# Attention core: how far the pass over the row maxima runs ahead of the scores

## The reference

```python
scores = jnp.einsum('bhqd,bhkd->bhqk', q, k) / jnp.sqrt(jnp.asarray(hd, x.dtype))
attn = jax.nn.softmax(scores, axis=-1)
out = jnp.einsum('bhqk,bhkd->bhqd', attn, v)
```

## Time and profile before

| | |
|---|---|
| time, median of 3 runs | 4916.33 us (4907.15 to 4920.6) |
| profiled execution, its own time | 4910.83 us, span 4909.0 us |
| busy of the span | PE 85%, DVE 59%, ACT 48%, POOL 28% |
| `pyr_core`, span of its pass A and B | about 322 to 535 us |
| `l1x_core` | about 1490 to 1898 us |
| `l2a_core` | about 2312 to 2520 us |
| `l3x_core` | about 4280 to 4803 us |

### The profile page before, as it was taken

The page is one execution under the profiler, slowest core; times in us unless marked ns, Lnnn a source line. Parts: engine busy times, 40 slices in busy tenths (PEclk is TensorE's granted clock), DMA queues, the critical chain, the costliest instruction groups (busy, mean ns, idle before and its releaser), DMA issues. The chain is left out here.

```text
span 4909.0 us, 69714 instructions
## 1 busy us (share of the span) xinstructions
PE 4175.8 (85%) x20384; PEld 1981.0 (40%) x20384; DVE 2875.6 (59%) x6517; ACT 2348.4 (48%) x4572; POOL 1358.6 (28%) x1202
## 2 busy tenths in 40 slices
PE   8779856689788997897979699999998988489986
PEld 6322445386552333573334233333335544222224
DVE  4558474401667884005861378787873256388866
ACT  4447331243244774333754355454552246269993
POOL 0122141211101111112110188787883212101112
PEclk9669988799887998897989799999999989689998
DMA  8545212354033332674335422111210034623421
GB/s 288 118 101 123 52 38 35 142 198 145 25 131 67 63 63 66 246 242 135 81 83 197 150 71 66 61 61 61 69 51 24 22 113 96 152 48 92 96 55 38
DMA packets 332041, 486.56 MB, mean 99 GB/s; under 512 B 84516, under 2 KB 232596, under 8 KB 317252
## 3 DMA queue, kind: packets, MB, share of 16 engines
q1 hardware_dynamic: 325008, 449.92, 32.2%
q0 software_dynamic: 6384, 32.61, 2.1%
q10 hardware_dynamic: 348, 0.44, 0.0%
HBM read 327.63 MB, written 143.92 MB: 96 GB/s over the span
## 5 line engine op out<-in xcount | busy, mean ns | idle before, releaser
L1356 POOL TENSOR_TENSOR lc_totals<-lc_totals,lc_weights 128x1024 f32<-128x1024 f32 (+1 forms) x320 | 623.0, 1947 | 165.9 <-DVE lc_totals L1305 134.8
L1265 ACT ACTIVATE lc_weights<-ps 128x1024 f32<-128x1024 f32 x384 | 393.2, 1024 | 447.1 <-PE ps L1182 436.8
L1286 DVE TENSOR_REDUCE lc_part_max<-ps 128x2 f32<-128x1024 f32 x384 | 466.1, 1214 | 206.4 <-PE ps L1162 204.0
L1182 PE MATMUL ps<-lc_q,lc_k 64*128 64x512 f32 x1536 | 398.1, 596 | 4.8 <-issue 4.8
L1192 PE MATMUL ps<-lc_weights,lc_v 128*64 128x512 f32 x1536 | 371.7, 605 | 0.0
L866 DVE TENSOR_REDUCE l1x_core_part_max<-ps 128x1 f32<-128x512 f32 x512 | 316.4, 681 | 55.4 <-PE ps L690 55.3
L862 DVE CUSTOM_DVE_ANT_0 l3x_core_unused<-ps,l3x_core_mask_q 128x512 f32<-128x512 f32 x512 | 330.6, 686 | 6.9 <-DVE l3x_core_row_max L870 4.9
L825 ACT ACTIVATE l3x_core_weights<-ps 128x512 f32<-128x512 f32 x512 | 327.6, 694 | 7.3 <-PE ps L758 7.0
L825 ACT ACTIVATE l1x_core_weights<-ps 128x512 f32<-128x512 f32 x512 | 266.1, 603 | 84.0 <-PE ps L758 83.8
L808 ACT ACTIVATE ps<-l3x_core_mask_k 128x512 f32<-128x512 f32 x384 | 270.7, 705 | 35.9 <-DMA l3x_core_mask_k<-in_mask_k 35.9
L690 PE MATMUL ps<-l3x_core_k,l3x_core_q 96*128 96x512 bf16 x512 | 214.2, 419 | 56.0 <-DVE l3x_core_part_max L862 40.8
(11 more groups left out here) (493 smaller groups left out, 8574.1 us busy)
## 6 DMA issues: line engine op xcount, KB each, us to landing
cf_w<-in_L1f_w SPq DMA_DIRECT2D x32, 1024.0 KB, 7.5
lc_k<-latent_k SPq DMA_DIRECT2D x32, 768.0 KB, 6.6
lc_v<-latent_values SPq DMA_DIRECT2D x32, 768.0 KB, 4.9
latent_k<-feed_staged SPq DMA_DIRECT2D x64, 256.0 KB, 2.6
latent_values<-feed_staged SPq DMA_DIRECT2D x64, 256.0 KB, 2.0
k_heads<-proj_parts SPq DMA_DIRECT2D x40, 384.0 KB, 2.6
q_heads<-proj_parts SPq DMA_DIRECT2D x32, 384.0 KB, 2.6
q_heads<-proj_parts SPq DMA_DIRECT2D x32, 256.0 KB, 3.0
```

Source lines behind the costliest of these rows:

```text
L1182: mm = nc.tensor.matmul(out[j], k_tile[g % RING][strip(j), i * P:(i + 1) * P], q_tile[g % RING][strip(j), :], start=False, stop=True)
L1265: nc.scalar.activation(weights[:, i % TILES, :, :], k.ps[:, B0 + (i % 2) * HEADS:B0 + (i % 2 + 1) * HEADS, 0:nq], ACT.Exp, scale=scale).th ...
L1286: nc.vector.reduce_max(own, k.ps[:, A0:A0 + HEADS, :], AX).then_inc(a_taken, 1)
L1356: nc.gpsimd.tensor_tensor(total, total, own, ALU.add).then_inc(added_by_pool, 1)
```

## The change

In stages with 16-channel heads that are neither causal nor cut into spans (`pyr_core`, `l1x_core`, `l2a_core`, `l3x_core`), pass A runs one group and three key tiles ahead in place of two groups (`EARLY = 3`). FRONT is 12 chunks for both sizes; the turn of the maxima comes at key tile TURN = nkt - 3 (1 for 512 keys, 5 for 1024), within it after the third head. `split_max` moves behind `normalise` in POOL's group, `row` to the end of SP's group (with a mask in group 3: before the last of the four mask tiles), and the mask rows for the next batch are loaded in group 2 in place of group 1. The other two stages keep their order.

```diff
-    def chunks_of(i):
-        some = list(range(i * NCH // nkt, (i + 1) * NCH // nkt))
-        return [some[len(some) * j // heads:len(some) * (j + 1) // heads] for j in range(heads)]
+    EARLY = 3 if small and not causal and spans is None else nkt
+    late_row = EARLY < nkt
+    FRONT, TURN = NCH * EARLY // nkt, nkt - EARLY
+    def chunks_at(s):
+        return [(1 + m // NCH, m % NCH) for m in range(FRONT + s * NCH // NS, FRONT + (s + 1) * NCH // NS)]
...
 SP, group(b, g):
-                if exists(*later(b, g, 1)):
+                if exists(*later(b, g, 1)) and not late_row:
                     row(*later(b, g, 1))
...
-                if mask is not None and g == groups - 3 and exists(b + 1, 0):
+                if mask is not None and g == groups - (2 if late_row else 3) and exists(b + 1, 0):
...
+                new_mask = mask is not None and g == groups - 1 and exists(b + 1, 0)
+                for i in range(nkt // 2 if new_mask else 0):
+                    if late_row and i == nkt // 2 - 1:
+                        row(*later(b, g, 1))
+                    sync.wait_ge(exp_done, at(b, g, NS, 2 * (i + 1) * heads + 3))
+                    load_mask_k(b + 1, i)
+                if exists(*later(b, g, 1)) and late_row and not new_mask:
+                    row(*later(b, g, 1))
...
 PE (DVE alike, with maxima for pass_a and negate for turn):
-            pass_a(0, 1, range(NCH))
+            pass_a(0, 1, range(FRONT))
...
-                        pass_a(*later(b, g, 2), more[j])
+                        for ahead, n in chunks_at(s):
+                            if exists(*later(b, g, ahead)):
+                                pass_a(*later(b, g, ahead), [n])
+                        if late_row and (i, j) == (TURN, heads - 2) and exists(*later(b, g, 1)):
+                            turn(*later(b, g, 1))
...
-                    if i == 0 and exists(*later(b, g, 1)):
+                    if not late_row and i == 0 and exists(*later(b, g, 1)):
                         turn(*later(b, g, 1))
...
 POOL, group(b, g):
-                    if small and i == 0 and exists(*later(b, g, 1)):
+                    if small and not late_row and i == 0 and exists(*later(b, g, 1)):
                         split_max(*later(b, g, 1))
...
                 if g >= 2 and to_finish(b - 1):
                     normalise(b - 1, 2 * g - 4)
                     normalise(b - 1, 2 * g - 3)
+                if late_row and exists(*later(b, g, 1)):
+                    split_max(*later(b, g, 1))
```

More of the change, by code:

```diff
@@ L745, in group @@
                 for i in range(nkt):
-                    more = chunks_of(i) if exists(*later(b, g, 2)) else [()] * heads
                     qs, ks = queries_of(i), slice(i * P, (i + 1) * P)
@@ L910, in _ @@
             negate(0, 0)
-            maxima(0, 1, range(NCH))
+            maxima(0, 1, range(FRONT))
             def group(b, g):
@@ L915, in group @@
                 for i in range(nkt):
-                    more = chunks_of(i) if exists(*later(b, g, 2)) else [()] * heads
                     for j in range(heads):
                         after = step_after(b, g, i * heads + j)
+                        if late_row and (i, j) == (TURN, heads - 1) and exists(*later(b, g, 1)):
+                            negate(*later(b, g, 1))
                         if after[2] in by_vector and exists(*after[:2]):
                             fill(*after, at(b, g, NS, i * heads + j + 3))
-                        maxima(*later(b, g, 2), more[j])
+                        for ahead, n in chunks_at(i * heads + j):
+                            if exists(*later(b, g, ahead)):
+                                maxima(*later(b, g, ahead), [n])
                         if (i, j) in inverse_at and not small and exists(*before):
                             invert(*before, inverse_at.index((i, j)))
-                    if i == 0 and exists(*later(b, g, 1)):
+                    if not late_row and i == 0 and exists(*later(b, g, 1)):
                         negate(*later(b, g, 1))
```

## The result

The changed kernel takes 4979.5 us (median of 4 runs, 4975.7 to 4980.9), the kernel before 4915.6 (4907.2 to 4920.6): ratio 1.0131, 95% interval 1.0113 to 1.0148. It is slower by 1.3%, some 64 us; 4950 was forecast, with 4905 to 4985 as the range. The profiled execution spans 4976.3 us against 4909.0, so +67.3.

The account below looks back on a forecast made before the run. PE was taken to set the steady pace, DVE the starts and ACT the ends. Terms -29.1 (start), -9.8 (mask), +59.1 (SP's extras), +19.5 (clock), -3.3 (an old stall gone) gave +36.4 us; forecast 4950, range 4905 to 4985.

Parts of the forecast that it names:

- What bounds the kernel: The four stages: PE sets the steady pace, DVE the start, ACT the last stretch; a stage's gain or loss is the kernel's.
- Shorter start: Fewer chunks ahead of the first score: `l1x_core` net 10.1 us, 512-key stages 2.0 each, `l3x_core` 15.0; sum -29.1.
- Mask rows moved: `l3x_core`: moving the mask transfer to group 2 removes DVE's gap at two loop turns, -9.8 us; 0 if the loop is slow.
- The row with 1024 keys: 1024-key stages: the later row of maxima still lands in time, cost 0, with 1.5 us of slack.
- SP's extras with 512 keys: `pyr_core` and `l2a_core`: SP's other work delays the row in groups 0, 1 and 3, and PE stands 59.1 us.
- The clock: 512-key stages: 1.2 GHz after stalls costs 1.5 us for each of 13, 19.5 in all; bounds 0 and 37.
- More than forecast: Rival: each stall starts the next group at 1.2 GHz and DVE's loop gap stays: +64 us, 4980; chance 0.13.
- Half the loss: Rival, 512-key stages: the row overtakes the inverses and the clock holds: +6 us, 4922; chance 0.15.
- SP's queue has room: Rival, 512-key stages: SP's extras cost less without the row's DMAs in front, losses 18 us, 4895; faster chance 0.10.
- Does not do what it says: Rival: 512-key stages have no late row, the only effect is the start: 4877; counted with the faster rival, chance 0.10.

Follow-up runs that it names:

- x1_long_only: The changed order kept only in the 1024-key stages, the 512-key stages as in the kernel before: 4882.7 us, ratio 0.9939 to the kernel before.
- x8_mask_late: The kernel before, with only the last mask load in `l3x_core` held back to the middle of the next group: 4907.9 us, ratio 0.9999.
- x9_two_tiles: `x1_long_only` with `EARLY = 2` in place of 3, so the turn comes one tile later: 4916.1 us, ratio 1.0016 to the kernel before.
- x5_inverses_last: The changed kernel with only group 1's `return_inverses` moved behind the row of maxima in the 512-key stages: 4943.0 us, ratio 1.0074 to the kernel before.

## Why the prediction was right, and where it was off

The sign and the mechanism were right: 64 us slower where 36 was the sum, for the reason given. The size was caught by the range, 4905 to 4985, and not by the sum: 4979.5 lies above the 4935 to 4970 that the forecast gave for its own mechanism, and 5 us below the upper end. Of the 31 us between the sum, +36.4, and the profiled +67.3, 16 lie inside the 512-key stages (5 of waits, 11 of clock), 10 inside `l3x_core`, where the mask term was, and 6 in the starts. All of these came out slower than forecast. Step by step:

- **What bounds the kernel.** Right. PE holds still in the 512-key groups, and what it waits is added to the stage. Only in the last stretch of `l1x_core` was "ACT had been the bound" too strong: PE is busy for 17.43 of the 20 us there, ACT for 17.22.
- **Shorter start.** `l1x_core`: -10.0 ahead and +2.65 back, -7.3 for -10.1. `l3x_core`: -16.8 for -15.0. The 2.0 each for the 512-key stages can't be seen in one execution (+1.4 and -0.4). `x1_long_only`, -27, is what these steps are worth with the next one.
- **Mask rows moved, -9.8.** The step failed: the cause was not the transfer but the turn of the loop, the end that I had priced at 0. The two long groups of the earlier trace rows stand 31.77 and 30.93 us apart after, against 33.57 and 33.66: 4.5 us went, of which the load, by `x8_mask_late`, is 1.1 at most. `l3x_core` gave that back, 2.7 us of it in its other groups and the rest at its end, where pass A now runs beside the exponentials, and comes out at +0.4; "nothing comes back" was wrong too.
- **The row with 1024 keys, 0 with 1.5 us of slack.** Right: no wait with three tiles, and `x9_two_tiles` puts the slack at 1.48.
- **SP's extras with 512 keys, 59.1 us.** Nearly right: 68.0, less 5.4 that the kernel before had already. By kind: group 0 took 2.1, 1.6 and 2.0 in `pyr_core` (forecast 1.9) and 2.0, 1.45, 0.7 in `l2a_core` (1.5). Group 3 took 4.2, 5.9 and 5.5 (5.5), and 5.2 and 4.9 (5.1). Group 1 took 6.3, 5.2 and 5.8 (4.6), and 6.3 and 5.4 (4.2). Two small waits of 1.8 and 1.5 in the last batch, where no loads are left, were not in the count. Group 1 was under by 1.2 in `pyr_core` and 1.7 in `l2a_core`, mainly because the inverses take 2.5 us to get out directly behind the loads, not the 1.55 of the earlier trace rows, where the row stood between.
- **The clock, 19.5 us.** This is the term that failed in size. The stages grew by 91.7 us, of which 62.6 are waits; 29.1 is left, and PE's busy time says 30.7. The count was nearly right: all ten waits of 4.19 us and more, and one of the eight of 2.10 and less, were followed by 1.2 GHz, so 11 for 13. The price was wrong: in the 8 us behind each of those 11, the granted clock averages 0.55 to 0.75, which is 2.0 to 3.6 us lost, 3.1 in the mean. I had read 1.5 from a single case behind a wait of 1.73 us; the 2.3 of my upper bound was nearer.
- **The rivals.** "More than forecast" gave 4980 and the measured time is that, for half of its reason (the dear clock, though not behind every stall); the loop's gap did shrink, and that won nothing. "Half the loss" fell on both its conditions: the row stays behind the inverses, and the clock falls. "SP's queue has room" fell: in the changed kernel the copies take 6.34 us. "Does not do what it says" fell.

## What to carry over

A transfer that is needed soonest must be issued first on its queue: moving the same work of SP from ahead of the row of maxima to behind it took 79 us off the changed kernel. When a deadline moves into the middle of a stage, add up what the issuing queue does between the old place and the new one and set that against the length of the group: with 23 us there were 1.5 to spare, with 11.7 there were none, and so the change pays only in the long stages (-27 us). Price a stall of TensorE with what comes behind it: here 3 us at the low clock on top of each wait over 4 us, half as much again.

## What was not expected of the hardware

- Waits of 0.72 to 2.05 us left the granted clock at 1.00 seven times over the next 8 us, while one of 2.10 us brought it to 0.50, as one of 1.73 did before. In `x5_inverses_last` one of 2.63 us left it at 1.00. The length of a short wait alone doesn't decide.
- Useless products that fill a wait shortened both stages, although 14 blocks of 4 us were added to PE.
- DVE stands for 3.1 us where a loop turns back with no transfer beside it, ACT for 2.39 us at the same turn of the changed kernel.
